# Causal attention with its value products issued for two key units at a time, on one Trainium2 core

## What is computed

```python
q = _rope(split_heads(x @ Wq.T), pos); k = _rope(split_heads(x @ Wk.T), pos); v = split_heads(x @ Wv.T)
score = jnp.einsum('bqd,bkd->bqk', q, k)
score = jnp.where(causal[None], score, -jnp.inf)
attn = jax.nn.softmax(score / jnp.sqrt(jnp.float32(D_K)), axis=-1)
out = jnp.einsum('bqk,bkd->bqd', attn, v)
# merged heads, then out @ Wo.T, added to x
```

## Time and profile before

| | |
|---|---|
| median of 3 runs | 973.03 us (964.84 to 975.87) |
| the profiled execution | 971.15 us, span 969.2 us |
| PE busy | 781.0 us, 81% of the span |
| DVE busy | 658.9 us, 68% |
| ACT busy | 530.0 us, 55% |
| POOL busy | 354.1 us, 37% |
| mean granted TensorE clock | 0.900 |

### The profile page before, as it was taken

The page is one execution under the profiler, slowest core; times in us unless marked ns, Lnnn a source line. Parts: engine busy times, 40 slices in busy tenths (PEclk is TensorE's granted clock), DMA queues, the critical chain, the costliest instruction groups (busy, mean ns, idle before and its releaser), DMA issues. The chain is left out here.

```text
span 969.2 us, 17210 instructions
## 1 busy us (share of the span) xinstructions
PE 781.0 (81%) x5494; PEld 426.3 (44%) x5494; DVE 658.9 (68%) x1821; ACT 530.0 (55%) x1126; POOL 354.1 (37%) x635
## 2 busy tenths in 40 slices
PE   2839777258459999999999999999999988578874
PEld 2838777234212333333333333333333337567773
DVE  4475565279867787787877878778787209656563
ACT  1206666215404667766677666766667643146663
POOL 5006777217812222332223322233222210047774
PEclk9659999769856999999999999999999779589998
DMA  9062222214572022210222102221020000532221
GB/s 323 34 174 71 76 74 72 64 36 116 155 189 35 2 50 52 50 44 10 50 51 51 43 10 50 51 50 43 10 51 3 1 1 1 146 81 73 78 77 24
DMA packets 42083, 62.32 MB, mean 64 GB/s; under 512 B 7843, under 2 KB 33453, under 8 KB 40592
## 3 DMA queue, kind: packets, MB, share of 16 engines
q1 hardware_dynamic: 33248, 45.76, 18.7%
q0 software_dynamic: 6240, 14.48, 5.6%
q10 hardware_dynamic: 2512, 1.06, 0.4%
HBM read 39.87 MB, written 21.92 MB: 64 GB/s over the span
## 5 line engine op out<-in xcount | busy, mean ns | idle before, releaser
L1235 DVE CUSTOM_DVE_ANT_0 cst<-psS,cst 128x768 bf16<-128x768 f32 (+7 forms) x512 | 364.4, 755 | 103.0 <-PE psS L1109 100.7
L1199 ACT ACTIVATE prob<-psST 128x512 f32<-128x512 f32 (+3 forms) x768 | 323.8, 495 | 143.3 <-PE psST L1134 139.8
L1148 PE MATMUL a_psO<-prob,vs 128*32 128x512 f32 (+3 forms) x1536 | 168.5, 511 | 0.9 <-POOL prob L1320 0.7
L1319 POOL TENSOR_TENSOR a_gate<-a_zeros 1x1 f32<-1x1 f32 x128 | 23.6, 184 | 335.1 <-ACT prob L1199 335.1
L1134 PE MATMUL psST<-a_qs,ks 75*128 75x512 bf16 (+1 forms) x480 | 123.9, 327 | 5.7 <-ACT prob L1199 3.3
L654 POOL DMA_INDIRECT g_row<-rows,f_there_number x78 | 77.8, 998 | 133.3 <-SPq L500 110.1
L1109 PE MATMUL psS<-ks,a_qs 72*128 72x512 bf16 (+2 forms) x480 | 116.6, 332 | 5.3 <-DVE a_rowmax L1235 5.2
L1109 PE MATMUL psS<-ks,qs 72*128 72x512 bf16 (+3 forms) x288 | 76.6, 359 | 24.5 <-DMA qs<-q_split 17.1
L555 PE MATMUL g_psH<-g_xnT,g_w1s 128*128 128x128 f32 x624 | 83.6, 277 | 2.4 <-ACT g_xnT L583 2.4
L1134 PE MATMUL psST<-qs,ks 75*128 75x512 bf16 (+3 forms) x288 | 80.3, 351 | 6.3 <-ACT prob L1199 5.1
L565 PE MATMUL g_psY<-g_w2s,g_hidT 128*128 128x128 f32 x624 | 83.4, 277 | 1.1 <-ACT g_hidT L590 1.1
(11 more groups left out here) (154 smaller groups left out, 923.0 us busy)
## 6 DMA issues: line engine op xcount, KB each, us to landing
ks<-k_split SPq DMA_DIRECT2D x48, 192.0 KB
rows<-tok SPq DMA_DIRECT2D x8, 1028.0 KB, 11.1
a_qs<-q_split SPq DMA_DIRECT2D x60, 96.0 KB
k_split<-p_part SPq DMA_DIRECT2D x40, 128.0 KB, 2.3
qs<-q_split SPq DMA_DIRECT2D x36, 96.0 KB
q_split<-p_part SPq DMA_DIRECT2D x24, 128.0 KB, 2.3
w<-in_Wb SPq DMA_DIRECT2D x1, 2064.0 KB, 10.7
w<-in_W SPq DMA_DIRECT2D x1, 2048.0 KB, 15.8
```

The costliest lines, as they stand in the source:

```text
L1148: last = nc.tensor.matmul(psO[32 * h:32 * h + 32, c0:c0 + w], vs[r][:, j, h, :], prob[:, u % RING, h, 0:w], start=(j == 0), stop=(u + 1 in ...
L1199: nc.scalar.activation(prob[:, u % RING, h, 0:w], psST[(u * QH + h) % 3][:, 0:w], ACT.Exp, scale=SCALE).then_inc(exp_done, 1)
L1235: last = nc.vector.tensor_tensor_reduce(out=out[:, a * CH:a * CH + width], in0=ps[:, a * CH:a * CH + width], in1=mask_row[:, S - width:], ...
```

## The change

`weigh` no longer stands behind the first score of every unit. It stands behind the first score of every second unit (u1, u3, ... u11), and then for two units in one go: u-3 and u-2. Units below zero are those of the stage before (u10, u11 behind u1's first score). The turning of chunk 0's output moves from the end of u5 to the end of u6, and both `copy_out` on ScalarE stand one unit later. Since `plan` deals the tiles by the account to which `weigh` adds, the tiles move too.

```diff
@@ plan
             for h in range(QH):
                 found.append(("score", u, h))
                 att += w
-                if h == 0:
-                    if u >= LAG:
-                        found.append(("weigh", u - LAG, 0))
-                        att += WEIGH_COST * units[u - LAG][3]
-                    elif not first:
-                        found.append(("weigh", u - LAG, 1))
-                        att += WEIGH_COST * units[u - LAG + UN][3]
+                if h == 0 and u % 2 == 1:
+                    for v in (u - LAG - 1, u - LAG):
+                        if v >= 0:
+                            found.append(("weigh", v, 0))
+                            att += WEIGH_COST * units[v][3]
+                        elif not first:
+                            found.append(("weigh", v, 1))
+                            att += WEIGH_COST * units[v + UN][3]
                 spread()
@@ EXTRAS
-    EXTRAS = [(1, "turn_max", 1, True), (4, "turn_out", 1, False), (5, "turn_out", 0, True),
+    EXTRAS = [(1, "turn_max", 1, True), (4, "turn_out", 1, False), (6, "turn_out", 0, True),
@@ ScalarE, stage
-                if u == 1 and not first:
+                if u == 2 and not first:
                     copy_out(s - 1, 1)
-                if u == half_end[0] + 1:
+                if u == half_end[0] + 2:
                     copy_out(s, 0)
                 exps(s, u)
```

## The result

The changed kernel takes 1083.93 us (median of 4, 1075.62 to 1087.10), the kernel before 968.93 in the same comparison: ratio 1.119, 95% interval 1.114 to 1.125. The forecast was 1038 in a range of 1008 to 1080: the sign was right, the size was not. Times are medians of all executions, ratios and their intervals are of the fast ones only: one of the six executions of experiment 6 took 3248.76 us at a mean clock of 0.22, one of experiment 8 took 1075.29 us, and both are left out of the ratios.

A forecast was written before the change was run, and what follows sets the result against it. TensorE was taken to set the pace of a 30.31 us stage: -1.2 for pairs, -2.8 old delays, +8.1 new ones, +4.1 in all. 15 stages +61, last +2, about 1036, plus 2 for the clock: 1038 us, range 1008 to 1080.

The forecast's parts named there:

- The walk through the queue: TensorE's new queue in one middle stage, by five rules: delays sum to 8.1 us against 2.8 before, stage 34.4 us.
- the single waits named above: TensorE late in u7, u8 and u2: T15 0.83 us, turn_max 0.27, T16 0.86, u2's fourth score 0.66.
- The saving of the pairs: Joined weighs on TensorE save 0.20 us a pair, six pairs a stage: -1.2 us a stage.
- The clock: The granted clock falls to half now and then, 7 us lost per 20.48 us fall; 2 us added in all.
- rival B: Waits as walked, and the clock falls in three to six stages or more: 1057 to 1080 us, chance 0.25.
- The Trainium skill's rule on the clock: Only long idle gaps between bursts take TensorE's clock back; the walk has none, so the sum would stay at 1036 us.
- The drain on a change of tiling mode: Changing tiling mode drains TensorE; each entry into and return from narrow matmuls costs 0.24 us, which the change halves.
- Rival D: Entries into narrow matmuls decide, new delays staying at the old 2.8 us a stage: 954 us, chance 0.05.
- A's range: Waits as walked, clock mostly full: 1038 us, or 1020 to 1052 if added waits are a quarter off; chance 0.55.
- C: Half the waits, DVE and ScalarE catching up earlier: about +1.8 us a stage, 1000 to 1015 us, chance 0.10.
- The copy's move: In u2 the copy-out stands ahead of the exponentials, 0.49 us more to the next; the fourth score waits 0.66.
- The last stage: ScalarE is waited for there; the late first exponential of odd units costs about 0.4 us a pair: +2 us.

The follow-up runs named there:

- experiment 6: The kernel before, single units kept, its 24 tiles put at places chosen by walking the queue for fewest waits: 946.69 us, ratio to before 0.977.
- experiment 8: The kernel before, single units, copies and turns kept, with the tiles at the places the change gives them: 1066.12 us on another chip, ratio 1.019.
- experiments 4: The kernel before with reductions and exponentials over half of their columns, so results are not the attention's: 930.06 us.
- experiment 5: The changed kernel with reductions and exponentials over half of their columns, so results are not the attention's: 941.53 us.
- Experiment 1: The changed kernel with 15 extra score matmuls a stage (the fill) where TensorE stood still: 1042.46 us, ratio to before 1.074.
- experiments 2: The changed kernel with pairs kept but the tiles dealt out by the old account: 1017.27 us, ratio to before 1.049.
- 6 to 9: Includes 7, the changed kernel with tiles placed by the walk: 961.9 us, ratio 0.992; and 9, Experiment 1 with ScalarE's copies moved back: 1118.37 us (another chip), 1.077.
- experiment 3: The changed kernel with the old account's tile places and the tile due at a pair ahead of it: 1016.34 us, ratio to before 1.048.

## Why the prediction missed its range

- **The walk through the queue: right.** It gave 34.4 us a stage at full clock; the measured one is 34.25 in the changed kernel and 34.24 with the fill, and the single waits named above agree to 0.02 us (T15, turn_max, T16, u2's fourth score).
- **The saving of the pairs: right, a little small.** 1.2 taken, 1.4 to 1.5 found (experiments 4 and 5); a pair lasts 1.85 us where 1.89 was expected (the walk has 1.98 for it in one place).
- **The clock: this step failed.** "I add 2 for the clock falling now and then" should have read about 50. 14 middle stages at 34.24 are 479.4 us, the measured ones 532.9: 53.5 us. Experiment 1 gives back 41 of it by holding the clock. The price of time at half clock was too low: I worked out 7 us per 20.5, that is 0.34 us lost for each; a fall of 3.4 us costs 1.64 (32.00 to 33.64), that is 0.48, and 53.5 us over the 122.9 us at half clock in the 14 stages are 0.44. But most of the miss is the amount: the 2 us stand for some 6 us at half clock, and there were 122.9, in 26 falls over the 15 stages with tiles, most of 3.4 us and five of 10.2. I had found the rows behind which the clock fell with no wait over 0.54 us in brackets and the place in my own walk that is no better. I then set it aside because dense pairs stand next to it. But the walk repeats 15 times: a thin place is met in every stage. The mechanism of rival B was the result, with shorter falls in all 15 stages instead of long ones in three to six; six of B's long ones would have been the same 123 us at half clock. The prediction's own sign of being wrong, long stretches at half clock between 303 and 757 us, came as well. The other terms together came out some 6 us under the forecast and hid a little of this.
- **The Trainium skill's rule on the clock** ("TensorE: Matmul & The Clock Gate", closing table), by which only long gaps take the clock back, does not cover this case. No gap ahead of 706.79 is over 0.9 us, and the clock fell. The measurement decides.
- **The drain on a change of tiling mode** (the Trainium skill, "TensorEngine Tiling (Array Packing)", Key Properties) agrees with the traces as far as they go: 0.24 us is lost per entry and return, and halving them does save. Rival D fell because the added waits (5.3 us a stage) are not under 1.2, as walked.
- **Two slips in the rivals' sums**, which decide nothing: a quarter of the added waits (5.3 us x 15 stages) is 20 us, so A's range should be 1018 to 1058; and half of them leaves +1.45 a stage, not +1.8, so C should be about 995.
- **The copy's move**: named, and worth 0.38 us a stage, inside the 0.66 at u2.
- **The last stage**: forecast +2, measured -2.8. The forecast mechanism is there: ScalarE now waits five times for the weigh that frees `prob`, 4.4 us in all, where it had no such wait before.

```profile
ACT prob L1200 <- PE a_psO L1149: 4.4, 5, 1.4
```

  But the stage has 6.8 us at half clock where it had 20.5, which I had not separated. At 0.44 to 0.48 us each that would be 6 us or more gained, so the pairs by themselves would have cost some 3 to 4; this is an estimate, and no run shows it.
- **Not settled**: why pairs and new places cost more together (3.9) than one by one (1.7 for the pairs with the copies' and `turn_out`'s moves, 1.4 for the places). My reading is that a pair lets DVE and ScalarE run dry and the cluster behind it has to wait for both, but no run takes the two apart further. Nor is it settled why the clock falls in some stages and not in others that have the same order and the same waits (experiments 2 and 8, and the two stretches of the changed kernel).

## What to carry to other kernels

Here an order in which the busiest engine is rarely late was worth more than fewer switches on it: between two uses of a double buffer there must be as much other work as the consumer takes (0.66 us stood against 1.22), and batching removes just that work. Walk the new queue by start-to-start distances read from the old trace before trusting a saving; here that gave stage lengths to 0.2 us for the change and four orders after it (6 to 9), and used forwards it gave a version 2.3% faster than the kernel before (1.7 to 3.0). Where the queue was not walked wait by wait it missed, by 1.0 us or more a stage in experiment 3 and by 2.7 in experiment 5 (26.3 expected, 29.01 measured). If the walk has a cluster of waits in a place that repeats, like the one behind which the old trace shows a fall, price the half clock for every repetition and not for a few.

## What the hardware showed that was not expected

- The clock fell behind stretches in which TensorE was busy 2.62 of 3.42 and 2.43 of 3.41 us, with no idle gap above 0.9 us by starts. In the late stages it was back at full after 3.41 us in which TensorE was busy throughout; in the last stage of the kernel before it had taken 20.48 us.
- More matmuls made the kernel faster: 15 idle-time copies a stage, 1083.93 to 1042.46 us.
- Four heads' narrow fp32 matmuls of a second unit join the first's with nearly no seam: 1.85 us for two, against 2 x 0.99 and an entry of 0.09 between them for two apart.
